# The state loop of a Mamba block: the product with B moves from GpSimd to the vector engine

## The reference

```python
Bm = h @ w_B.T + b_B                    # (4, 1024, 16)
Cm = h @ w_C.T + b_C
Delta = softplus((h @ w_d1.T + b_d1) @ w_d2.T + b_d2)
A_bar = exp(-Delta[..., None] * A)      # 16 states for each of 128 channels
BX = (Delta * h)[..., None] * Bm[:, :, None, :]
_, states = associative_scan(comb, (A_bar, BX), axis=1)   # s[t] = A_bar[t] * s[t-1] + BX[t]
y = einsum('blfn,bln->blf', states, Cm) + D * h
g = y * silu(h0)
```

## Time and profile before

| | |
|---|---|
| median of 3 runs | 2756.42 us (2756.4 to 2757.33) |
| span of the profiled execution | 2757.4 us |
| TensorE, matmul | 2292.2 us busy (83%) |
| VectorE | 2103.8 us (76%) |
| GpSimd | 1243.0 us (45%) |
| ScalarE | 1162.1 us (42%) |
| mean granted clock of TensorE | 0.901 |
| GpSimd, L538 (`bx`) | 64 instructions, 171.4 us |
| VectorE, L964 (scan) | 64 instructions, 207.4 us |

### The profile page before, as it was taken

How to read it: one execution, slowest core, us unless ns; L and a number is a source line. 1 busy time by engine, 2 the same in 40 slices (tenths; PEclk the granted TensorE clock), 3 DMA queues, 4 the chain that set the end, 5 groups by cost and what they waited for, 6 DMA issues and landing times.

```text
span 2757.4 us, 45423 instructions
## 1 busy us (share of the span) xinstructions
PE 2292.2 (83%) x11606; PEld 1361.5 (49%) x11606; DVE 2103.8 (76%) x3267; ACT 1162.1 (42%) x1889; POOL 1243.0 (45%) x1058
## 2 busy tenths in 40 slices
PE   3649999879665999997966599999796669999889
PEld 1235555547323555554732455564572245555456
DVE  4868888769496888876948688886794878888678
ACT  3413443337541434344743143443474223434256
POOL 2544555433253646443325465554333455556332
PEclk9779999989886999998978799999897879999889
DMA  1000000001000000000100000000100000000011
GB/s 56 0 23 5 5 8 4 0 19 41 11 0 23 5 9 4 4 0 25 36 9 0 23 5 9 4 4 1 31 30 9 0 23 5 8 8 0 3 34 33
DMA packets 36374, 35.84 MB, mean 13 GB/s; under 512 B 4008, under 2 KB 31120, under 8 KB 36240
## 3 DMA queue, kind: packets, MB, share of 16 engines
q1 hardware_dynamic: 36240, 34.27, 4.2%
HBM read 32.16 MB, written 2.10 MB: 12 GB/s over the span
## 4 chain that ended last, share of the span: by engine, by line
PE 58%; DVE 18%; issue 10%; ACT 7%; POOL 5%; DVEq 1%; ACTq 0%; DMA 0%; POOLq 0%; SPq 0%
PE ps L1431 8%; PE ps L1446 7%; PE ps L1216 6%; PE ps L1217 5%; PE ps L1218 5%; PE ps L1413 4%; DVE state L964 4%; PE ps L1415 3%; PE ps L1332 3%; PE ps L1286 3%; POOL bx L538 3%; PE ps L1491 2%; ACT q_split L750 2%; PE ps L1244 2%; DVE inverse L1007 2%
## 5 line engine op out<-in xcount | busy, mean ns | idle before, releaser
L767 ACT ACTIVATE probs<-ps 128x512 f32<-128x512 f32 (+3 forms) x768 | 356.5, 488 | 510.8 <-PE ps L1418 282.0
L1071 DVE TENSOR_REDUCE tops<-ps 128x1 f32<-128x512 f32 (+3 forms) x768 | 387.7, 545 | 116.7 <-PE ps L1446 81.7
L612 POOL TENSOR_TENSOR prob_sums<-prob_sums,probs 128x512 f32<-128x512 f32 (+3 forms) x256 | 237.8, 929 | 334.4 <-ACT probs L767 322.5
L1446 PE MATMUL ps<-k_high,q_split 128*128 128x512 f32 (+3 forms) x768 | 323.0, 435 | 41.9 <-POOL k_high L484 35.0
L1413 PE MATMUL ps<-q_split,k_high 128*128 128x512 f32 (+3 forms) x768 | 324.5, 423 | 21.8 <-ACT probs L767 15.5
L1431 PE MATMUL ps<-probs,vals 128*64 128x512 f32 (+3 forms) x1536 | 325.4, 509 | 0.0
L1415 PE MATMUL ps<-q_max,k_low 65*128 65x512 f32 (+7 forms) x768 | 268.9, 350 | 0.0
L1446 PEld LDWEIGHTS ps<-k_high,q_split 128*128 128x128 f32 x768 | 159.1, 208 | 218.0 <-issue 112.0
L574 POOL TENSOR_TENSOR roped<-turned 128x1024 f32<-128x1024 f32 x64 | 155.4, 2429 | 239.2 <-DVE turned L1048 226.3
L538 POOL TENSOR_TENSOR bx<-du,b_rows 128x1024 f32<-128x1024 f32 x64 | 171.4, 2691 | 199.9 <-ACT b_rows L712 163.8
L964 DVE TENSOR_TENSOR_SCAN state<-decay,bx 128x1024 f32<-128x1024 f32 x64 | 207.4, 3240 | 42.9 <-POOL bx L538 42.9
(11 more groups left out here) (230 smaller groups left out, 4937.6 us busy)
## 6 DMA issues: line engine op xcount, KB each, us to landing
w<-in_w SPq DMA_DIRECT2D x128, 128.0 KB, 2.1
w_pair<-in_w_pairs SPq DMA_DIRECT2D x36, 256.0 KB, 2.6
xin<-in_x SPq DMA_DIRECT2D x5, 512.0 KB, 3.8
out<-acc SPq DMA_DIRECT2D x4, 512.0 KB, 4.1
pos<-in_c_pos SPq DMA_DIRECT2D x1, 512.0 KB, 4.8
v_w<-in_v_w SPq DMA_DIRECT2D x1, 512.0 KB
o_w<-in_o_w SPq DMA_DIRECT2D x1, 512.0 KB
v_b<-in_v_b SPq DMA_DIRECT2D x1, 512.0 KB
```

Source lines behind the costliest of these rows:

```text
L612: pool.tensor_tensor(total, before, probs[:, u % RING, 1, at:HALF], ALU.add).then_inc(p_added, 1)
L767: act.activation(probs[:, u % RING, h, q0 - HALF * c:HALF], ps[:, 4 + h, 0:w], ACT.Exp, scale=SCALE).then_inc(blocks_taken, 1)
L1071: dve.tensor_reduce(tops[:, h, u:u + 1], ps[:, MX_BANK[u % 3], 0:w], AX_X, ALU.max).then_inc(scores_taken, 1)
L1446: made = pe.matmul(o, q_split[par][h][:, i * P:(i + 1) * P], k_high[par][h][:, k0:k0 + w], start=True, stop=not own)
```

## The change

GpSimd does nothing in the loop any more. VectorE makes `bx` itself, and reads the broadcast of B from the PSUM banks, so that ScalarE's copy and the tile `b_rows` are gone. VectorE's order becomes scan(n), `drive`(n+1) (the product `bx`), `weigh`(n) (the product `cs`). TensorE's broadcast of B waits until the product that reads the banks is done (`bx_ready`), and comes one place later in the order: B(n+1), C(n+1), add(n). ScalarE keeps the exponential.

```diff
-        b_rows = sb("b_rows", [P, 2, SEQ], F32, m_ctx)
...
-        b_bcast, b_taken, c_bcast = sem("b_bcast"), sem("b_taken"), sem("c_bcast")
+        b_bcast, c_bcast = sem("b_bcast"), sem("c_bcast")
...
-        CREDITS = [(proj_out, 2 * 10), (y_stored, 16), (a_taken, 2), (v_taken, 2), (scanned, 2), (bx_ready, 2),
-                   (cs_used, 2), (b_taken, 1), (cs_ready, 2),
+        CREDITS = [(proj_out, 2 * 10), (y_stored, 16), (a_taken, 2), (v_taken, 2), (scanned, 2), (bx_ready, 1),
+                   (cs_used, 2), (cs_ready, 2),
...
@@ GpSimd @@
-                pool.wait_ge(delta_ready, b + 1)
-                pool.sem_inc(passed, 1)
-                with pool.Fori(0, STATES // 2) as r:
-                    for k in range(2):
-                        n = b * STATES + 2 * r + k
-                        pool.wait_ge(b_taken, n + 2)
-
-                        pool.wait_ge(scanned, n + 1)
-                        pool.tensor_tensor(bx[:, k, :], du[:, :], b_rows[:, k, :], ALU.mult).then_inc(bx_ready, 1)
...
@@ ScalarE @@
+                act.wait_ge(delta_ready, b + 1)
+                act.wait_ge(a_taken, b * A_OUTS + 12 + 2)
+                act.sem_inc(passed, 1)
                 with act.Fori(0, STATES // 2) as r:
                     for k in range(2):
                         n = b * STATES + 2 * r + k
-                        act.wait_ge(b_bcast, n + 1)
-
-                        act.wait_ge(bx_ready, n + 1)
-                        act.activation(b_rows[:, k, :], banks(2), ACT.Copy).then_inc(b_taken, 1)
-                        act.wait_ge(delta_ready, b + 1)
-
                         act.wait_ge(scanned, n + 1)
-                        act.sem_inc(passed, 1)
                         act.activation(decay[:, k, :], delta[:, :], ACT.Exp,
                                        scale=neg_a[:, bass.ds(2 * r + k, 1)]).then_inc(decay_ready, 1)
...
@@ VectorE @@
-                with dve.Fori(0, STATES // 2) as r:
+                dve.wait_ge(delta_ready, b + 1)
+
+                def drive(n, k):
+
+                    dve.wait_ge(b_bcast, n + 1)
+
+                    dve.wait_ge(scanned, n + 1)
+                    dve.tensor_tensor(bx[:, k, :], du[:, :], banks(2), ALU.mult).then_inc(bx_ready, 1)
+
+                def scan(n, k):
+                    dve.wait_ge(bx_ready, n + 2)
+                    dve.wait_ge(decay_ready, n + 1)
+
+                    dve.wait_ge(cs_ready, n + 1)
+                    dve.tensor_tensor_scan(state[:, k, :], decay[:, k, :], bx[:, k, :], 0.0, ALU.mult, ALU.add
+                                           ).then_inc(scanned, 1)
+
+                def weigh(n, k):
+                    dve.wait_ge(scanned, n + 3)
+                    dve.wait_ge(c_bcast, n + 1)
+
+                    dve.wait_ge(cs_used, n + 1)
+                    dve.tensor_tensor(cs[:, k, :], state[:, k, :], banks(4), ALU.mult).then_inc(cs_ready, 1)
+
+                drive(b * STATES, 0)
+                with dve.Fori(0, STATES // 2 - 1) as r:
                     for k in range(2):
                         n = b * STATES + 2 * r + k
...
+                        scan(n, k)
+                        drive(n + 1, 1 - k)
+                        weigh(n, k)
+                scan(b * STATES + STATES - 2, 0)
+                drive(b * STATES + STATES - 1, 1)
+                weigh(b * STATES + STATES - 2, 0)
+                scan(b * STATES + STATES - 1, 1)
+                weigh(b * STATES + STATES - 1, 1)
...
@@ TensorE @@
                 def broadcast_b(i):
 
-                    pe.wait_ge(b_taken, b * STATES + i + 1)
+                    pe.wait_ge(bx_ready, b * STATES + i + 1)
...
                 broadcast_b(0)
-                broadcast_b(1)
                 broadcast_c(0)
                 with pe.Fori(0, STATES // 2 - 1) as r:
                     for k in range(2):
-                        broadcast_b(2 * r + k + 2)
+                        broadcast_b(2 * r + k + 1)
                         broadcast_c(2 * r + k + 1)
                         add_state(2 * r + k, k)
+                broadcast_b(STATES - 1)
                 broadcast_c(STATES - 1)
                 add_state(STATES - 2, 0)
                 add_state(STATES - 1, 1)
```

## The result

The changed kernel takes 2865.68 us (2865.07 to 2866.77), the kernel before on the same chip 2756.88 (2756.4 to 2759.24): a ratio of 1.0392, with a 95% interval of 1.0378 to 1.0407. It is slower by 109 us; forecast were 99.5 us more, and 2856 us.

A forecast was written before the change was run, and what follows sets the result against it. TensorE was taken as busiest, with GpSimd's product and the scan on the state loop's path. Blocks of 7.45 + 96.32 + 3.46 + 2.8 = 110.0 us, four 440.1 against 340.6, +99.5, gave 2856 us; range 2820 to 2900.

The forecast's parts named there:

- ring: State loop: TensorE's C, additions and B, then `bx`, `cs`, and again; 6.88 us a state, bounds 5.30 and 7.83.
- Until the first `cs` ends: Start of a block, from the end of `du` through the first `cs`: 7.45 us.
- Fourteen rounds: Middle of a block, until `cs`(14): 14 rounds of 6.88 us, 96.32 us.
- The last state: End of a block, scan and `cs` with no `bx` after: 2.20 + 0.04 + 1.22 = 3.46 us.
- The last additions: End of a block, from the last `cs` to `hc`: 2.8 us, between about 2.0 fast and 3.63 slow.
- Outside the blocks: Rest of the run: TensorE's clock levels may fall otherwise, some us in all; otherwise as before within 2 or 3 us.
- Scans at 2.28 us, none held up: VectorE in the loop: with GpSimd's products gone, every scan takes 2.28 us, against a mean of 3.24 before.
- Other edits free: ScalarE's exponential, GpSimd's shorter stream and one more VectorE wait cost nothing, lying beside other work.
- The clock: TensorE in the loop: after 2.5 us without work nearly every burst starts slow and rises on its way.
- The clock kept: Rival, 10%: TensorE's clock stays up, 5.30 us a state, 87.9 a block, +11.0 us, 2767; partly kept, 2790 to 2830.
- The clock never back: Rival, 8%: bursts that start slow stay slow, 7.83 us a state, 124.1 a block, +155.8 us, 2912.
- VectorE's pace: Rival, 5%: TensorE delivers B during the scan, 4.48 us a state, 76.4 a block, −34.9 us, 2721.

The follow-up runs named there:

- e3_fill6: The changed kernel with six matmuls into an unread bank after each B in the loop: 2784.79 us, 1.0098 of the kernel before.
- e2_b_second: The changed kernel with TensorE's loop order C(n+1), B(n+2), add(n), so B ahead of the additions: 2717.29 us, 0.9853 of the kernel before.
- e6_fill3: The changed kernel with three matmuls into an unread bank after each B in the loop: 2838.47 us, 1.0297 of the kernel before.

## Why the prediction was right

The mechanism was the one forecast: the late B closes a ring, and the gap in it costs the fast clock in every state. The number came out 9.8 us too low, in terms that were each a little off. By the prediction's own steps, first block, forecast against measured.

- *Until the first `cs` ends*: 7.45, measured 74.68 − 67.51 = 7.17. Here TensorE began B(0) sooner after `du` than before.
- *Fourteen rounds*: 6.88 each, 96.32. Measured (171.88 − 73.47) / 14 = 7.03, together 98.4. The ring is the one described, link by link. The 6.88 came from a single burst, low for some 3.2 us of its course. The first two rounds after were 7.83 and 7.73, slow nearly throughout, which is the other bound; then 6.98 or 6.99 five times in a row, and on down to 6.83 towards the end of the block. That one burst gave the mean to 0.15 us was in part luck. This term was 2.1 us too low; the first and the last one were too high by 0.8 together, so a block came out 1.3 too low.
- *The last state*: 3.46, measured 176.55 − 173.10 = 3.45.
- *The last additions*: 2.8 between two bounds, measured 178.81 − 176.55 = 2.26, near the fast one.
- *Outside the blocks*: "some us in all", measured 1.9 us. The median lies 2.5 us over the span of the profiled execution, where the prediction took it 1.0 us under. That step failed because the two are different measures, and because the profiled execution of the kernel before was 2.4 us above its median. The blocks with 4.4 (444.5 for 440.1), the rest with 1.9 and this with 3.5 are the 9.8 us between 2855.9 and 2865.7.
- *Scans at 2.28 us, none held up*: so measured. *Other edits free*: no run tests them alone; the 1.9 us outside the blocks leave little room for a price. In the loop ScalarE waited only for scans.
- *The clock*: forecast that nearly every burst starts slow and rises on its way. Measured in the first block: the level goes up and down once a state. The first two bursts are slow nearly throughout, the next two begin fast and fall half a microsecond in, two more fall during C, and the last eight start slow and rise on their way, as forecast. The slow part of a burst has much the same length wherever it lies, 3.1 to 3.4 us, and so the cost was right for the last twelve; the first two cost 0.8 to 0.9 us more each.
- *The rivals.* The clock kept: it happens with gaps of 1.24 us [e3_fill6] and 1.69 us [e2_b_second], in some rounds with 1.89 [e6_fill3], and never with 2.54. The rule of the Trainium skill, TensorE: Matmul & The Clock Gate, section "HAM oscillation — how this bites in real kernels", would have kept it with 1.89 and 2.54 as well; the measurement decides against it. So the 1.99 us gap of the earlier trace rows was the right row to go by. The clock never back: only in the first one or two rounds of a block. VectorE's pace: it is what the loop would do with B in time, 4.44 us measured for 4.48 worked out, and 2725 or 2717 us for 2721.

How the 103.9 us divide follows from the experiments. Without the late B the blocks are 37.5 us cheaper than before (340.6 to 303.1). The late B costs 141.4 (303.1 to 444.5). Of these 56.8 are there with six matmuls in the gap (303.1 to 359.9), 10 of them from the slow first rounds; so the ring itself costs some 47, and the level of the clock some 95. This split is an estimate: it takes the six matmuls as free.

## What to carry to other kernels

When work is moved to another engine, write down for each wait which instruction of the other engine stands ahead of the one waited for. Here a gain on GpSimd and VectorE worth 38 us in the blocks was turned into a loss of 104 by one place in TensorE's order, and with B ahead of the additions again the gain is back. A loop that passes between TensorE and VectorE in turn, without overlap, paid twice here: for the sum of both, and for the clock that TensorE lost by gaps of 2.5 us.

## What the runs showed of the hardware that was not expected

- Adding matmuls whose result nobody reads shortened the run by 81 us (six a state) and 27 us (three a state).
- The level can fall in the middle of a burst that works without a break, half a microsecond after a gap of 2.54 us has ended (1.00 until 97.8, 0.50 from 98.0).
- A GpSimd product of 2.35 us beside the scans costs 0.2 us a state or 1.2, by its start alone. A VectorE sum of two SBUF tiles that takes 0.28 us alone took 1.87 us behind a GpSimd instruction.
- The place of the fall moves through the burst from round to round, while the period goes from 7.83 us over 6.99 to 6.83 and stays there.
